# A Mamba layer with a recurrent feed-forward on one core: scans from a constant with the carry added to their first token, and products for two columns in one GpSimd instruction

## What is computed

```python
xz = x_in @ W_in
x, z = (xz[..., :D], xz[..., D:])
proj = x @ W_x                      # D columns for delta, N = 16 for B, 16 for C
delta = softplus(proj[..., :D] @ W_dt + b_dt)
A = -exp(A_log)
dA = exp(einsum('bld,dn->bldn', delta, A))
dBx = einsum('bld,bln->bldn', delta * x, B_ssm)
def step(h, inp):                   # over the 2048 tokens of a sequence, from h = 0
    dA_t, dBx_t, C_t = inp
    h = dA_t * h + dBx_t
    y_t = einsum('bdn,bn->bd', h, C_t)
    return (h, y_t)
y = ys + x * D_param
y = y * silu(z) @ W_out
res = y + x_in
return layernorm(res) * ln_g + ln_b
```

## Time and profile before

| | us |
|---|---|
| median of 3 runs | 943.9 (942.05 to 944.43) |
| the profiled execution, its own time | 944.42 |
| its span, first to last instruction | 942.6 |

### The profile page before, as it was taken

How to read it: one execution, slowest core, us unless ns; L and a number is a source line. 1 busy time by engine, 2 the same in 40 slices (tenths; PEclk the granted TensorE clock), 3 DMA queues, 4 the chain that set the end, 5 groups by cost and what they waited for, 6 DMA issues and landing times.

```text
span 942.6 us, 15838 instructions
## 1 busy us (share of the span) xinstructions
PE 864.2 (92%) x5024; PEld 688.7 (73%) x5024; DVE 900.9 (96%) x985; ACT 847.9 (90%) x2064; POOL 889.1 (94%) x399
## 2 busy tenths in 40 slices
PE   8757679999999899989999899998999999999998
PEld 5545567877878587787868678786778768778876
DVE  4899989999999999999999999999999999999896
ACT  5886988989999999998999999999999999978875
POOL 4999999999999999999999989999999999999970
PEclk9987898999999999999999999999999999999999
DMA  7445435462534644455463644446354354446231
GB/s 222 156 177 204 175 138 204 179 235 104 210 157 161 239 164 172 183 178 166 174 248 147 224 148 160 179 179 248 125 210 179 143 198 179 157 160 223 91 101 45
DMA packets 49938, 163.60 MB, mean 174 GB/s; under 512 B 5248, under 2 KB 33152, under 8 KB 33600
## 3 DMA queue, kind: packets, MB, share of 16 engines
q1 hardware_dynamic: 48528, 161.27, 46.2%
q0 software_dynamic: 512, 1.31, 0.5%
q10 hardware_dynamic: 816, 0.02, 0.1%
HBM read 153.15 MB, written 9.44 MB: 172 GB/s over the span
## 4 chain that ended last, share of the span: by engine, by line
PE 46%; ACT 28%; DVE 15%; issue 9%; DMA 1%; POOL 0%; POOLq 0%; DVEq 0%; SPq 0%; ACTq 0%
PE w_ps L1326 10%; ACT da_ps L654 10%; PE y_ps L1317 9%; PE w_ps L1350 6%; DVE da_ps L1033 5%; PE w_ps L1359 4%; PE w_ps L1362 4%; DVE hg L1049 3%; DVE hg L1033 3%; PE w_ps L1465 3%; DVE hg L1040 2%; PE w_ps L1368 2%; ACT xn_tok L591 2%; ACT h_tok L591 2%; ACT zs L715 2%
## 5 line engine op out<-in xcount | busy, mean ns | idle before, releaser
L542 POOL TENSOR_TENSOR dbx<-u,b_ring 128x1024 f32<-128x1024 f32 x255 | 599.4, 2380 | 4.7 <-DVE hg L1033 4.6
L654 ACT ACTIVATE da_ps<-delta,a_neg 128x512 f32<-128x512 f32 x512 | 340.0, 684 | 23.9 <-DVE hg L1040 7.3
L555 POOL TENSOR_TENSOR hg<-hg,c_ring 128x1024 f32<-128x1024 f32 x122 | 290.4, 2381 | 8.5 <-ACT carry L660 6.7
L1317 PE MATMUL y_ps<-ident,hg 128*128 128x128 f32 x2048 | 264.3, 279 | 9.2 <-POOL hg L555 9.0
L1317 PEld LDWEIGHTS y_ps<-ident,hg 128*128 128x128 f32 x2048 | 241.7, 145 | 35.9 <-issue 17.8
L1033 DVE TENSOR_TENSOR_SCAN da_ps<-da_ps,carry,dbx 128x512 f32<-128x512 f32 x203 | 249.8, 1271 | 4.3 <-ACT da_ps L654 4.1
L1033 DVE TENSOR_TENSOR_SCAN hg<-da_ps,carry,dbx 128x512 f32<-128x512 f32 x181 | 220.3, 1263 | 1.4 <-ACT carry L660 1.2
L1040 DVE TENSOR_TENSOR hg<-da_ps,c_ring 128x1024 f32<-128x1024 f32 x68 | 82.3, 1210 | 0.2
L1049 DVE TENSOR_TENSOR hg<-da_ps,c_ring 128x512 f32<-128x512 f32 x130 | 82.3, 673 | 0.0
L1033 DVE TENSOR_TENSOR_SCAN da_ps<-da_ps,dbx 128x512 f32<-128x512 f32 x64 | 75.8, 1213 | 3.3 <-ACT da_ps L654 2.8
L1326 PE MATMUL w_ps<-xnT_ring,w_in 128*128 128x512 f32 x120 | 61.4, 636 | 16.0 <-ACT xT L696 14.1
(11 more groups left out here) (212 smaller groups left out, 1333.0 us busy)
## 6 DMA issues: line engine op xcount, KB each, us to landing
c_ring<-bc_rows_dram SPq DMA_DIRECT2D x64, 1024.0 KB, 4.7
b_ring<-bc_rows_dram SPq DMA_DIRECT2D x63, 1024.0 KB, 6.7
xres<-in_L_attn_x_in_dram SPq DMA_DIRECT2D x16, 512.0 KB, 4.8
x_tok<-in_L_attn_x_in_dram SPq DMA_DIRECT2D x15, 512.0 KB, 5.9
out_dram<-r_out SPq DMA_DIRECT2D x14, 512.0 KB, 3.2
bc_rows_dram<-bc_rows SPq DMA_DIRECT2D x64, 16.0 KB, 5.4
w_in<-in_L_attn_W_in_dram SPq DMA_DIRECT2D x2, 256.0 KB, 4.3
x_tok<-in_L_attn_x_in_dram SPq DMA_DIRECT2D x2, 256.0 KB, 4.6
```

Source lines behind the costliest of these rows:

```text
L542: pool.tensor_tensor(dbx[:, n % X_RING, :, :], u[:, ip, :, :], b.to_broadcast([P, KH, LC]), ALU.mult).then_inc(s["dbx_done"], 1)
L555: pool.tensor_tensor(part, part, c_of(n).to_broadcast([P, KH, LC]), ALU.mult).then_inc(s["g_pool"], 1)
L654: act.activation(da_of(n, h), delta[:, ip, h, :], ACT.Exp, scale=a_neg[:, h, n:n + 1]).then_inc(s["da_ready"], 1)
L1317: last = pe.matmul(y_tok[:, b, h * P:(h + 1) * P], hg[:, n % H_RING, h, b * P:(b + 1) * P], ident[:, :], is_transpose=True, start=n == 0 a ...
```

## The change

Scans never read `carry`. ACT makes `first_a`, the decays of a block's first token, once for all 16 columns (`first_decays`, two exponentials of 16 elements, in the twelve blocks before one that has carries). VectorE multiplies it with `carry` for four columns at a time (`weigh_carries`, two columns ahead) and adds the product to the first token of `dbx` for two columns at a time (`hand_over`, one column ahead). Both stand between the two scans of a column. GpSimd makes `dbx` for two columns in one instruction of 2048 elements, in a ring of 6, four columns ahead. The tables of order and of banks are changed in some entries, and two loads on SP's queue change places. Semaphores of the last block that came in pairs are merged; their waits are the same.

```diff
-X_RING = 4
+X_RING = 6
+HAND = 2
+C_RUN = 1
-B_LEAD, C_LAG, Y_LAG = 3, 1, 2
+B_LEAD, C_LAG, Y_LAG = 4, 1, 2
...
-ACT_TURN = dict(... z0=11, z1=11, ... ln_exp=20, ...)
+ACT_TURN = dict(... z0=11, z1=12, ... ln_exp=21, ...)
-VEC_TURN = dict(... z0=12, ...)
+VEC_TURN = dict(... z0=13, ...)
-PE_TURN = dict(... xa1=9, xa0=9, xD=10, v0=12, v1=12, xo0=13, xo1=13)
+PE_TURN = dict(... xa1=9, xa0=8, xD=15, v0=10, v1=11, xo0=13, xo1=13)
...
+        first_a = sb("first_a", P, 2, NS, KH)
+        handed = sb("handed", P, NS, KH)
...
@@ SP's queue
                 if scan:
+                    load_b(t, 2)
                     if not (t == 0):
                         load_c(t, 1)
                 if more:
                     need(sp, s["xn_done"], t + 2)
                     sp.dma_start(x_tok[:, :, :], x_v[t + 2]).then_inc(s["x_loaded"], 16)
                 if scan:
-                    load_b(t, 2)
+                    load_b(t, 3)
                     load_c(t, 2)
-                    load_b(t, 3)
...
@@ GpSimd
+            def times_b_twice(i, ip, n):
+                need(pool, b_loaded[n // GN], 16 * (i + 1))
+                for m in range(KH):
+                    need(pool, s[f"u{m}_done"], i + 1)
+                need(pool, s["scan_done"], KH * (NS * i + n + 1 - X_RING + 1))
+                at, row = dbx_of(i, n), n % GN
+                b = b_ring[:, n // GN % BG, row:row + 2, :]
+                pool.tensor_tensor(dbx[:, at:at + 2, :, :], u[:, ip, :, :].unsqueeze(1).to_broadcast([P, 2, KH, LC]),
+                                   b.unsqueeze(2).to_broadcast([P, 2, KH, LC]), ALU.mult).then_inc(s["dbx_done"], 2)
...
@@ ACT
+            def first_decays(i, ip):
+                need_all_read(act, i - 1, ["dt0", "dt1"])
+                for h in range(KH):
+                    act.activation(first_a[:, ip, :, h], a_neg[:, h, :], ACT.Exp,
+                                   scale=delta[:, ip, h, 0:1]).then_inc(s["first_a_set"], 1)
...
                         act.preload_act_table_set(EXP_TANH)
+                        if (t + 1) % CPB:
+                            first_decays(t + 1, nxt)
...
@@ VectorE
+            def weigh_carries(i, ip, n):
+                part = slice(n, n + GN)
+                need(dve, s["first_a_set"], KH * firsts(i))
+                need(dve, s["carry_split"], kept_splits(i - 1, n + GN - 1))
+                need(dve, s["carry_saved"], kept_wholes(i - 1, n + GN - 1))
+                dve.tensor_tensor(handed[:, part, :], carry[:, part, :], first_a[:, ip, part, :],
+                                  ALU.mult).then_inc(s["handed_set"], 1)
+
+            def hand_over(i, ip, n):
+                dve.wait_ge(s["dbx_done"], NS * i + n + HAND)
+                dve.wait_ge(s["handed_set"], GROUPS * (firsts(i) - 1) + n // GN + 1)
+                at = dbx_of(i, n)
+                first = dbx[:, at:at + HAND, :, 0]
+                dve.tensor_tensor(first, first, handed[:, n:n + HAND, :], ALU.add).then_inc(s["handed_over"], 1)
...
-                first = t % CPB == 0
-                if not first and n in split_of(t - 1):
-                    need(dve, s["carry_split"], kept_splits(t - 1, n))
-                elif not first:
-                    need(dve, s["carry_saved"], kept_wholes(t - 1, n))
+                if t % CPB:
+                    dve.wait_ge(s["handed_over"], pairs_before(t) + n // HAND + 1)
...
-                    dve.tensor_tensor_scan(out, da_of(n, h), dbx[:, n % X_RING, h, :],
-                                           0.0 if first else carry[:, n, h:h + 1], ALU.mult, ALU.add).then_inc(s["scan_done"], 1)
+                    dve.tensor_tensor_scan(out, da_of(n, h), dbx[:, dbx_of(t, n), h, :],
+                                           0.0, ALU.mult, ALU.add).then_inc(s["scan_done"], 1)
+                    if h == 0:
+                        ahead = column_at(t, par, n + 1, True, pre, False)
+                        if ahead and ahead[0] % CPB and ahead[2] % HAND == 0:
+                            hand_over(*ahead)
+                        ahead = column_at(t, par, n + 2, True, pre, False)
+                        if ahead and ahead[0] % CPB and ahead[2] % GN == 0:
+                            weigh_carries(*ahead)
```

More of the change, by code:

```diff
@@ L362, in column_at, with c_of, dbx_of, products_of @@
             return (t, par, n) if scan else None
-        def c_of(n):
-            return c_ring[:, n // GN % BG, n % GN:n % GN + 1, :]
+        def c_of(n, k=1):
+            return c_ring[:, n // GN % BG, n % GN:n % GN + k, :]
+        def dbx_of(i, n):
+            return (NS * i + n) % X_RING
+        def products_of(i):
+            runs = []
+            for n in whole_of(i):
+                if i == LAST and n == NS - 1:
+                    break
+                if runs and len(runs[-1]) < C_RUN and runs[-1][-1] == n - 1 and n % GN:
+                    runs[-1].append(n)
+                else:
+                    runs.append([n])
+            return runs
         def da_of(n, h):
@@ L411, in column_before, with firsts, pairs_before @@
             return (i, at) if at >= 0 else (i - 1, at + NS)
+        def firsts(i):
+            return sum(1 for j in range(i + 1) if j % CPB)
+        def pairs_before(i):
+            return NS // HAND * (firsts(i) - 1)
         @block.sync
@@ L473, in step @@
                     load_b(t + 1, 0, start)
+                if scan:
+                    load_c(t, 3)
+                if pre:
+                    if not start:
+                        load_b(t + 1, 1)
                     load_c(t + 1, 0, start)
-                    load_b(t + 1, 1, start)
                     if start:
+                        load_b(0, 1, True)
                         load_c(0, 1, True)
```

94 lines of the change are left out of this document (47 added, 47 removed).

## The result

The changed kernel takes **1146.7 us** (median of 5 runs, 1145.5 to 1152.8) where the kernel before takes 942.7 (5 runs beside them): a ratio of 1.2174, 95% interval 1.2151 to 1.2197. The forecast was 940.0 with a range of 927 to 953, so it is wrong by 207 us; what happened is the first rival, which stood at 1130 with a chance of 0.18. All medians and ratios here are of fast executions: one of the kernel before (1774.0 us) and one of the scans alone with less on GpSimd (1775.0) took nearly twice as long and are left out.

The account below looks back on a forecast made before the run. VectorE was taken to set the pace, with GpSimd right behind. Scans -22.1, small operations +11.5, ACT +4.6, a wait saved -0.6 and given back +2.4 sum to -4.2 against 944.4: 940.2, given as 940, range 927 to 953.

Parts of the forecast that it names:

- the first rival: VectorE's small operations wait for GpSimd's instruction to end: products 161 us, additions 29, time 1130; chance 0.18.
- the price of the small operations: VectorE, between a column's two scans: 144 additions and products at 0.08 us each, +11.5 us, bounds 5.8 to 23.
- the fast kind: VectorE instructions from SBUF to SBUF taking 406 ns for 512 elements, against 674 from PSUM; two-input ones held not to belong.
- Scans: VectorE: 384 scans lose the pointer operand, 58 or 57 ns each, -22.1 us.
- Given back: VectorE: part of the saving turns into idle time, 0.2 us in each of 12 blocks, +2.4 us, bounds 0 and 5.
- ACT: `first_decays` behind the second table load: two small exponentials in 12 blocks, 0.38 us each block, directly on the path, +4.6 us.
- Pairs: GpSimd's `dbx` for two columns: 4.55 us against 4.66, 14 us less over the kernel, worth 0 on the time.
- Tables and loads: Changed entries of the order tables and swapped loads on SP's queue: no change in amount of work, 0.
- Waits for the pair: VectorE's additions waiting for GpSimd's pair: wanted 11.9 us after it can start, so 0.
- rival 3: PE falls behind through later `hg` products, its chain to ACT late: 2.2 us in half of 15 blocks, +16, 956; chance 0.04.

Follow-up runs that it names:

- the scans alone with less on GpSimd: Changed kernel's pairs, every scan from 0.0, nothing carried, no small operations or `first_decays`; column 3 of even blocks also split to VectorE: 935.5 us, ratio 0.9928 to the kernel before.
- the run with reductions: Changed kernel with each of the 144 small VectorE operations made a one-input reduction, SBUF to SBUF, carry not handed on: 939.4 us, ratio 0.9960 to the kernel before.
- the one without small operations and without `first_decays`: Changed kernel's pairs on GpSimd, every scan from 0.0, nothing carried between blocks: 934.3 us, ratio 0.9896 to the kernel before.
- single products on GpSimd: Changed kernel with GpSimd's `dbx` products one column at a time again, all 144 small operations kept: 1032.8 us, ratio 1.0937 to the kernel before.
- the multiply by a constant: Changed kernel with the 144 small operations as `tensor_scalar` by 1.0, one SBUF input, carry not handed on: 1139.6 us, ratio 1.2092 to the kernel before.
- the additions from PSUM: Changed kernel with only the 96 additions reading one input from PSUM, products keeping two SBUF inputs, carry left out: 1106.7 us, ratio 1.1713 to the kernel before.
- the run with groups of eight columns: Changed kernel with GpSimd making the small operations, products for eight columns, column 3 of even blocks split to VectorE: 942.5 us, ratio 0.9993 to the kernel before.

## Why the prediction was wrong

**The step that failed** is the price of the small operations, "I take the distance of the starts, since neighbouring scans overlap in the same way: 144 x 0.08 = +11.5", together with its bounds, 5.8 to 23, which came from two instructions that had no GpSimd beside them. Measured: 224.7 us of busy time. Two kernels with the small operations in the same places put a price on the waiting for GpSimd: 1.2174 with two inputs, 0.9960 with the reduction, 0.221 or **209 us**. The block of 356.00 says the same by itself. Its small operations in the changed kernel:

```profile
L1074 DVE TENSOR_TENSOR handed<-carry,first_a 128x8 f32<-128x8 f32 x4 | 14.5, 3621 | 0.0
...
L1083 DVE TENSOR_TENSOR dbx<-dbx,handed 128x4 f32<-128x4 f32 x8 | 5.9, 732 | 0.0
```

and the same block in the run with reductions:

```profile
301.26:357.24 55.98, 53.20 (x315) 41.75 (x314) 55.04 (x72) 53.73 (x139) 52.54 (x16) 1.00 0.50 180
```

20.4 us of small operations there (some 1.7 of them when nothing blocks), and 76.16 - 55.98 = 20.2 us between the two blocks: in this block what VectorE loses, the kernel loses.

The prediction did find the mechanism, as a rival, and its total came near: 1130 (measured 1146.7). Its products were right, 48 x 3.35 = 161 of wait (157.8 with their own length, about 151 without); its additions were not, 29 (66.9, about 53 without their own length). What went wrong is the **choice**. "None with both inputs in SBUF ran beside GpSimd. All 144 new ones would": the rows were silent on this case, and I took their silence for the forecast, though the one meeting that they held was a wait to the other's end. The argument against, that a two-input instruction isn't of the fast kind, says nothing of how it reads its second input. Nor was the small size any protection: an addition of 4 elements took up to 2323 ns and a product of 8 up to 10582. The term that decides here is a count times what is left of a GpSimd instruction (144, and up to 4.5 us each), and the upper bound of the small operations, 23 us, had to contain it.

**The other terms**, one by one:

- *Scans*, -22.1: the lengths are right, 1211 and 1207 ns. *Given back*, +2.4, was too small: alone, pairs and constant scans bring 9.6, so 12.5 are given back (give or take about 2). The prediction's first reading, "So VectorE sets the pace", doesn't hold in every block. I scaled the idle time of VectorE in the block of constants and overlooked why it idles: GpSimd (54.27 of 54.50) has no room below 54.1 to 54.4 us in the blocks of even number, and with constant scans these stop there, at no idle time of GpSimd. The block after each start of a sequence falls only from 55.95 to 55.5; what limits it wasn't found. In the kernel before, one of the six blocks of the earlier trace rows has GpSimd full already, with VectorE at 54.98 of 55.70:

```profile
357.80:413.50 55.70, 53.48 (x314) 43.40 (x313) 54.98 (x58) 53.45 (x137) 55.70 (x25) 0.97 0.49 181
```

- *ACT*, +4.6: 4.55, give or take 2.2.
- *Small operations, when not blocked*: a scan starts 0.05 us after a small operation does, not 0.08. The run with reductions is at a ratio of 0.9960, the one without small operations and without `first_decays` at 0.9896: 6.0 us, of which ACT is 4.55, so about 1.5 for the 144, give or take 3 (all four intervals together). By duration they are 21.1 us on VectorE and by the distance of starts 144 x 0.05 = 7.2; that the rest fell into idle time which GpSimd's limit had left is likely, but no run shows it.
- *Pairs*, 4.55 against 4.66, worth 0: 4.54 and a ratio of 1.0000. *Tables and loads*, 0: the same run.
- *Waits for the pair*, 0: 2.4 us in the changed kernel, where everything is late anyway; 0.2 with the reductions.
- *PE behind later products* (rival 3): `y_ps` waits 9.9 us for these products now, 9.0 before.

So with small operations that don't wait for GpSimd the kernel stands at 939.4, and 940.2 was forecast. That is luck: two errors that cancel, some 10 us too much hoped of the scans and some 10 too much charged to the small operations.

## What to carry to other kernels

Before an operation is put on VectorE between others, ask what GpSimd does meanwhile, however small the operation: in these runs a VectorE instruction with two inputs in SBUF, or a `tensor_scalar` from SBUF to SBUF, waited at least until GpSimd's current instruction ended, and longer GpSimd instructions made it wait longer. Such a wait stands in the profile as a long duration without idle time before it: compare the minimum, median and maximum of the line, then lay the two timelines beside each other. With one input in PSUM, or as a reduction, an operation of the same size takes 0.15 us beside GpSimd (151 and 155 ns, 144 and 151). And where a rule speaks of exactly the case that the trace doesn't show, one run of the case is cheap, and a range that leaves it out is too narrow.

## What was unexpected

- The wait can pass over whole instructions. One product started at 73.58, 0.75 us into the first of two pairs back to back, and wasn't let in between them, nor after the second, but only with the end of the third instruction. GpSimd, then VectorE:

```profile
72.83 9.01 POOL L582 TENSOR_TENSOR dbx<-u,b_ring 128x2048 f32<-128x2048 f32 x2
81.80 2.35 POOL L597 TENSOR_TENSOR hg<-hg,c_ring 128x1024 f32<-128x1024 f32 x1
```

```profile
73.58 10.58 DVE L1074 TENSOR_TENSOR handed<-carry,first_a 128x8 f32<-128x8 f32 x1
```

  It ended at 84.16, as the product `hg` of 81.80 did. Three other runs have such cases too: with single products on GpSimd a product of carries waited past the ends of five instructions (11849 ns) and an addition past one (3685), with the multiply by a constant one waited past two (10119), and with the additions from PSUM one product past two (10557) and one past one (5815). Everywhere else in the changed kernel VectorE was let in where one GpSimd instruction ended, also where the next stood right behind it (626.59 above); what makes the difference wasn't tried.
- In the scans themselves, which read `dbx` in SBUF and the decays in PSUM, nothing of the kind is seen, with or without the pointer in SBUF: beside a GpSimd that is busy 94% of the span, the 384 scans with a pointer have a mean of 1271 and 1263 ns, 58 more than without, so the pointer isn't treated as a second input.
- A small operation on GpSimd takes 213 ns (4 elements) or 218 (8), and 232 with 16 (in the run with groups of eight columns): hardly anything of it is the elements.
